# Rotary embedding of queries and keys: one VectorE product with both tables, the halves exchanged by DMA instead of ScalarE, GpSimd left with the sum

## The reference

```python
x = x + xattn(layernorm(x), ctx, ctx, mask, Wq, Wk, Wv, Wo)
x = x + ffn(layernorm(x), w1, w2, w3)

def apply_rope(x):                      # x: (b, t, h, 128)
    inv_freq = 1.0 / 10000.0 ** (arange(0, 128, 2) / 128)
    phase = tile(arange(t)[:, None] * inv_freq[None, :], (1, 2))
    return x * cos(phase) + rotate_half(x) * sin(phase)   # rotate_half: (-x2, x1)

# xattn: x is (8, 128, 512), 32 query heads, 8 key/value heads, 128 wide
q = apply_rope(query @ Wq); k = apply_rope(key @ Wk); v = value @ Wv
logits = 30 * tanh(q.k * 0.088388 / 30); weights = softmax(where(mask, logits, -1e30))
out = (weights @ v) @ Wo
# ffn: w1, w2, w3 are first quantised to the 16 values of NF4 in blocks of 64 and scaled back
out = (silu(x @ dq(w1).T) * (x @ dq(w2).T)) @ dq(w3).T
```

## Time and profile before

| | us |
|---|---|
| median of 3 runs | 922.24 (921.41 to 922.72) |
| the profiled execution's own time | 921.3 |
| its span, first to last instruction | 919.3 |
| busy: PE, PEld | 823.1, 650.1 |
| busy: DVE, ACT, POOL | 679.2, 534.9, 634.7 |
| mean granted TensorE clock | 0.964 of full |

### The profile page before, as it was taken

How to read it: one execution, slowest core, us unless ns; L and a number is a source line. 1 busy time by engine, 2 the same in 40 slices (tenths; PEclk the granted TensorE clock), 3 DMA queues, 4 the chain that set the end, 5 groups by cost and what they waited for, 6 DMA issues and landing times.

```text
span 919.3 us, 10659 instructions
## 1 busy us (share of the span) xinstructions
PE 823.1 (90%) x3806; PEld 650.1 (71%) x3806; DVE 679.2 (74%) x793; ACT 534.9 (58%) x681; POOL 634.7 (69%) x352
## 2 busy tenths in 40 slices
PE   3688798799899899899899899899877899998998
PEld 2467585677677677677677677677555688887886
DVE  8999969487677677677677677687698789896120
ACT  1266478477588488577577577577554266463100
POOL 4778549899899898898898898898720334434000
PEclk9899899799999999999999999999899999999999
DMA  8213453311311311312312212211200310403210
GB/s 315 98 51 115 146 181 108 104 35 46 121 35 47 120 35 49 118 35 56 110 35 70 98 37 82 83 45 44 78 0 32 101 46 3 153 1 100 55 58 35
DMA packets 49140, 70.83 MB, mean 77 GB/s; under 512 B 4160, under 2 KB 25792, under 8 KB 49088
## 3 DMA queue, kind: packets, MB, share of 16 engines
q1 hardware_dynamic: 49088, 70.15, 23.4%
HBM read 51.00 MB, written 19.14 MB: 76 GB/s over the span
## 4 chain that ended last, share of the span: by engine, by line
PE 53%; POOL 20%; DVE 17%; issue 5%; ACT 5%; DMA 0%; POOLq 0%; DVEq 0%; SPq 0%; ACTq 0%
POOL qT L1085 6%; DVE nfa L807 4%; PE bank L397 4%; PE bank L395 4%; PE bank L396 4%; PE bank L415 4%; PE bank L414 4%; PE bank L413 4%; POOL sw L1081 4%; PE bank L429 4%; PE avp L493 4%; PE bank L431 4%; PE bank L430 4%; PE bank L482 3%; PE trp L402 3%
## 5 line engine op out<-in xcount | busy, mean ns | idle before, releaser
L807 DVE SCALAR_TENSOR_TENSOR nfa<-nfp,nfa 128x1408 f32<-128x1408 uint8 x168 | 326.6, 1944 | 99.8 <-ACT nfp L624 98.6
L624 ACT ACTIVATE nfp<-nfv,bnd 128x1408 uint8<-128x1408 f32 x180 | 256.0, 1460 | 61.5 <-POOL nfv L1103 51.1
L1085 POOL TENSOR_TENSOR qT<-qT,sw 128x512 f32<-128x512 f32 x80 | 165.3, 2066 | 34.9 <-DVE qT L814 25.1
L631 ACT ACTIVATE sw<-bank 64x512 f32<-64x512 f32 x80 | 47.5, 594 | 139.5 <-PE bank L415 93.1
L429 PE MATMUL bank<-woh,ath 128*128 128x512 f32 x256 | 110.5, 432 | 0.0
L413 PE MATMUL bank<-xh,wqh 128*128 128x512 f32 x256 | 107.9, 422 | 0.0
L1137 POOL TENSOR_TENSOR eb<-eb,maskf 128x512 f32<-128x512 f32 x64 | 92.6, 1448 | 17.8 <-ACT eb L686 17.8
L431 PE MATMUL bank<-woh,atl 128*128 128x512 f32 x256 | 104.4, 408 | 0.0
L430 PE MATMUL bank<-wol,ath 128*128 128x512 f32 x256 | 104.3, 407 | 0.0
L414 PE MATMUL bank<-xl,wqh 128*128 128x512 f32 x256 | 103.0, 402 | 0.0
L415 PE MATMUL bank<-xh,wql 128*128 128x512 f32 x256 | 103.0, 402 | 0.0
(11 more groups left out here) (120 smaller groups left out, 1664.9 us busy)
## 6 DMA issues: line engine op xcount, KB each, us to landing
dq_scratch<-nfa SPq DMA_DIRECT2D x12, 704.0 KB, 3.1
stage<-wq_pieces SPq DMA_DIRECT2D x32, 256.0 KB, 2.9
stage<-wo_pieces SPq DMA_DIRECT2D x32, 256.0 KB, 2.6
stage<-dq_scratch SPq DMA_DIRECT2D x32, 256.0 KB, 3.2
nfv<-nf_rest SPq DMA_DIRECT2D x7, 704.0 KB, 4.1
ks_scratch<-qT SPq DMA_DIRECT2D x16, 256.0 KB, 2.1
vs_scratch<-vst SPq DMA_DIRECT2D x16, 256.0 KB, 2.4
kcur<-ks_scratch SPq DMA_DIRECT2D x16, 256.0 KB, 2.9
```

Source lines behind the costliest of these rows:

```text
L624: nc.scalar.activation(nfp[:, i % 2, :], nfv[:, :], ACT.Sign, bias=bnd[:, i:i + 1])\
L807: op = nc.vector.scalar_tensor_tensor(nfa[:, :], nfp[:, b % 2, :], STEPS[b], nfa[:, :], ALU.mult, ALU.add)
L1085: nc.gpsimd.tensor_tensor(dst, dst, sw[:, slot, :], ALU.add).then_inc(roped, 1)
```

## The change

- ACT's two copies per unit are gone (160 instructions).
- DVE's `rope_parts` multiplies the PSUM bank by both tables in one instruction, 128 x 2 x 512, into `products`, a new SBUF buffer of two slots (`cs_start` for the keys and the first six queries, `cs_loop` for the rest). It now waits for the bank itself (`proj_done`) and for the sum of the unit two before.
- SP's `swap` waits for the products (`cs_done`) and copies the sine product's halves, exchanged, from SBUF to SBUF into `sw`: two DMAs of 64 partitions x 512, 128 KB each. They stand in SP's one queue, in written order.
- POOL's `rope` waits for both DMAs (32 on the slot's semaphore) and adds the cosine product and `sw` into `qT`. The sine multiplications (80 instructions) are gone. The sign table changes sides, since it is now applied before the exchange.
- Waits that protect `qT` from being overwritten move from DVE to POOL. The key stores and first pieces in SP's queue are written in another order around the swaps.

```diff
-            def cos_part(ru, slot, dst, cos):
-
-                dve.wait_ge(swapped, ru + 1)
-                nc.vector.tensor_tensor(dst.rearrange("p (b t) -> p b t", b=4),
-                                        prj[slot][:, :].rearrange("p (b t) -> p b t", b=4), batches(cos), ALU.mult)\
-                    .then_inc(cos_done, 1)
+            def rope_parts(ru, slot, both):
+
+                dve.wait_ge(proj_done, ru + 1)
+                wait(dve, roped, ru - 1)
+                nc.vector.tensor_tensor(
+                    products(ru, slot).rearrange("p c (b t) -> p c b t", b=4),
+                    prj[slot][:, :].rearrange("p (o b t) -> p o b t", o=1, b=4).to_broadcast([128, 2, 4, S]),
+                    both.rearrange("p c (o t) -> p c o t", o=1).to_broadcast([128, 2, 4, S]), ALU.mult)\
+                    .then_inc(cs_done, 1)
...
-            def swap(ru, slot):
-
-                act.wait_ge(proj_done, ru + 1)
-                wait(act, roped, ru - 1)
-                nc.scalar.activation(sw[0:64, slot, :], prj[slot][64:128, :], ACT.Copy)
-                nc.scalar.activation(sw[64:128, slot, :], prj[slot][0:64, :], ACT.Copy).then_inc(swapped, 1)
...
+            def swap(ru, slot):
+
+                sp.wait_ge(cs_done, ru + 1)
+                wait(sp, roped, ru - 1)
+                part = products(ru, slot)
+                sp.dma_start(sw[0:64, slot, :], part[64:128, 1, :]).then_inc(swapped[slot], 16)
+                sp.dma_start(sw[64:128, slot, :], part[0:64, 1, :]).then_inc(swapped[slot], 16)
...
-            def rope(ru, slot, dst, sin):
-
-                pool.wait_ge(swapped, ru + 1)
-                part = sw[:, slot, :].rearrange("p (b t) -> p b t", b=4)
-                nc.gpsimd.tensor_tensor(part, part, sin.rearrange("p (o t) -> p o t", o=1).to_broadcast([128, 4, S]),
-                                        ALU.mult).then_inc(sin_done, 1)
-                pool.wait_ge(cos_done, ru + 1)
-                pool.wait_ge(sin_done, ru + 1)
-                nc.gpsimd.tensor_tensor(dst, dst, sw[:, slot, :], ALU.add).then_inc(roped, 1)
+            def rope(ru, slot, dst):
+
+                pool.wait_ge(cs_done, ru + 1)
+                pool.wait_ge(swapped[slot], 32 * (ru // 2 + 1))
+                nc.gpsimd.tensor_tensor(dst, products(ru, slot)[:, 0, :], sw[:, slot, :], ALU.add).then_inc(roped, 1)
```

In SP's `head(kv)`, with j = 8 kv:

```diff
                 nf_store(dq3[:, CH:2 * CH] if kv == 0 else dq12[:, (kv - 1) * CH:kv * CH], kv + 1)
-                head_piece(8 * kv + 4)
+                query_swap(j + AHEAD)
+                head_piece(j + 4)
+                query_swap(j + AHEAD + 1)
...
+                head_piece(j + 5)
+                query_swap(j + AHEAD + 2)
+                head_piece(j + 6)
+                query_swap(j + AHEAD + 3)
+                head_piece(j + 7)
...
+                query_swap(j + AHEAD + 4)
+                head_piece(j + 8)
+                query_swap(j + AHEAD + 5)
...
+                head_piece(j + 9)
+                query_swap(j + AHEAD + 6)
+                head_piece(j + 10)
+                query_swap(j + AHEAD + 7)
```

More of the change, by code:

```diff
@@ L119, in build @@
             ctl = sb("ctl", [128, KT, TOK], f32r, context)
+        with ExitStack() as loop:
+            cs_loop = sb("cs_loop", [128, 2, 2, 512], f32, loop)
         sb("ffn_place", [128, 6144])
         woh1 = sb("woh1", [128, G, D], f32r)
+        with ExitStack() as start:
+            cs_start = sb("cs_start", [128, 2, 2, 512], f32, start)
         wol1 = sb("wol1", [128, G, D], f32r)
@@ L179, in build, with products @@
         NF_STEPS = 20
+        def products(ru, slot):
+            return (cs_start if ru < NK + AHEAD else cs_loop)[:, slot, :, :]
         def split(eng, n):
@@ L281, in _ @@
             nf_load(nf_first[:, 0:CH], 0)
+            swap(0, 0)
+            swap(1, 1)
             for n in range(16, 20):
                 first_piece(n)
[L284 to L289, removed]
+            k_store(0)
+            for u in range(2, NK):
+                swap(u, u % 2)
+                k_store(u - 1)
+                if u in (9, 12):
+                    for n in (20, 21) if u == 9 else (22, 23):
+                        first_piece(n)
+            k_store(NK - 1)
             for n in range(24, 28):
@@ L442, in _ @@
                     split(pe, 16)
-                wait(pe, cos_done, u - 1)
+                wait(pe, cs_done, u - 1)
                 cs = slice(half * 512, (half + 1) * 512)
@@ L654, in _ @@
             for u in range(NK):
-                swap(u, u % 2)
                 if 6 <= u < 14:
@@ L696, in head @@
                         high(32 + j)
-                    if j + AHEAD < NUNIT:
-                        swap(NK + j + AHEAD, (j + AHEAD) % 2)
                     if j + 2 < NSTEP:
@@ L1123, in query_rope @@
             def query_rope(u):
-                _, half, g = unit_parts(u)
-                rope(NK + u, u % 2, qT[:, half, g, :], sinq[:, :])
+                kv, half, g = unit_parts(u)
+                if u < 8:
+                    pool.wait_ge(k_out[u], 32)
+                else:
+                    pool.wait_ge(logits_done, 8 * (kv - 1) + 4 * half + 4)
+                rope(NK + u, u % 2, qT[:, half, g, :])
             for u in range(AHEAD):
```

63 lines of the change are left out of this document (27 added, 36 removed).

## The result

| | before | after |
|---|---|---|
| median of 20 runs each | 922.07 us | 919.69 us |
| ratio, 95% interval | | 0.9979, 0.997 to 0.9989 |
| profiled execution, span | 919.3 us | 917.3 us |
| granted clock, mean | 0.964 | 0.972 |
| busy PE, DVE, ACT, POOL | 823, 679, 535, 635 us | 820, 699, 439, 465 us |

A forecast was written before the change was run, and what follows sets the result against it. It took PE and POOL to run level in a head, POOL's order setting most of the head's end. Seven heads at +2.7 (+19), keys 0, first queries -3: +16 on 921.3, so 938 us as median; range 906 to 966.

The forecast's parts named there:

- what is added on SP, and this decides: Swaps on SP in a head's steps: each unit takes 8.4 us against PE's 7.74, so 2.6 us more a head.
- the ring: In a head's steps: low part, piece, two swaps issued and landed, sum, mask, next low part; 8.4 us a unit.
- The head's end: Three stretches from step 5's logits to the second sum behind: 18.9, 11.4 and 6.8 us; changes +1.4, -1.6, +0.3.
- The last head: The head that loads no pieces and projects two units; left out of the +2.7 us booked for each of seven heads.
- Issue of the swaps: SP's time to issue a swap: assumed 0.33 us each, like a piece, with 0.04 between.
- Landing: From the second swap's issue to its landing: taken as 2.1 us, like the key stores, with ends 1.6 and 2.8.
- Keys: Key stage, 18 to 92 us: DVE's longer products against less lengthening by POOL; booked 0, between +8.5 and -10 us.
- First queries: POOL's first masks, for which PE waits 7.32 us, begin at 162.0 instead of 164.69: -3 us (0 to -7).
- no change: Rival: both L807 mostly hide in POOL's gap, 7.7 us a unit, gains and losses at the ends cancel: 922 us, chance 0.07.
- Relief wins: Rival: swaps land in 1.6 us, hidden under PE's step; heads -8, keys -4, first queries -4: 906 us, chance 0.22.
- DVE alone: Rival: nothing comes back in the key stage and heads hide the transfer; +8.5 - 3: 928 us, chance 0.07.
- the rule weighed in the prediction: Skill's rule: two half-partition DMAs gain almost nothing over one after the other; its rival, serial swaps: 972 us, chance 0.14.

The follow-up runs named there:

- e1: The changed kernel with each step's pair of swaps issued on SP behind the piece that waits for that step's low part: 1007.7 us, ratio 1.094.
- e3: The kernel before without POOL's product with the sine (left out of the computation), everything else as it was: 900.2 us, ratio 0.977.
- e12: The kernel before with DVE's cosine product of step 7 made behind the first of its three NF4 adds: 916.8 us, ratio 0.994.
- e9: The changed kernel with DVE's rotation product of step 7 behind the first of its three NF4 adds instead of the second: 902.0 us, ratio 0.978.
- e7: The changed kernel with the halves exchanged by two ScalarE copies instead of the two DMAs, and e9's edit: 1074.8 us, ratio 1.165.

## Why the prediction was wrong

**The step that failed** is the one called "what is added on SP, and this decides": "the piece waits for the low part of the same step", a ring of 8.4 us a unit, +2.6 us a head, +18 in seven heads. The piece that waits for a step's low part stands *behind* that step's swaps; the piece ahead of them waits for the low part of one step earlier, since it refills the slot used four pieces before. The text ahead of the prediction says "three before it" and "in the same step", and is wrong in both. The trace shows it: the swap follows the product by 0.02 us, and SP has sent the piece long before. e1, in which the ring is made, has 9.1 us a unit where the prediction had 8.4, and heads of 80.5 us. From the end of the next head's second sum at 385.73 to the logits of its step 5 at 416.83 are 31.1 us; before, 31.1 too (389.70 to 420.82). Forecast: 2.6 more.

**The head's end was right**, to a few tenths. From the logits of step 5 to the end of step 7's sum: 18.9 forecast, 368.13 - 348.98 = 19.15. To the mask behind the next sum: 11.4 forecast, 11.4 measured. To the next sum's end: 6.8 forecast, 385.73 - 379.50 = 6.2 measured. ACT's planes were to come 0.3 us earlier: from step 5's logits to the add ahead of the product were 365.08 - 352.69 = 12.4 us, now 361.09 - 348.98 = 12.1. Without the ring the prediction's own terms give +0.1 us a head. This head came out at -0.3, the mean of six within 0.1 of none. With the ring left out of the sum, the prediction would have read about 920 us (921.3 + 7 x 0.1 - 3 + 0.9). That this is the time measured is luck in part: the keys gave 1.6 us that were not booked, and the first and the last head lost 1.3 and 2.2 that were not booked either.

**The last head** was left out of the sum, and there the exchange is waited for most plainly. Its second sum starts at 656.62, after 3.02 us of waiting for its transfer, and PE waits for it in turn:

```profile
657.94 2.08 PE L518 MATMUL bank<-qT,kcur 128*128 128x512 f32 x2 [3.12 <-POOL qT L1097]
```

Before, the same wait was 1.48 us.

**The product** was put at 1.21 us: 1.20 to 1.22. **Issue of the swaps** at 0.33 each: 0.46 and 0.60, too low. **Landing** at 2.1, and 3.0 from product to sum: 2.2 to 2.3, and 3.0.

**Keys** were booked at 0: behind them, among the values, the second chunk's maxima start at 114.32 instead of 115.91, so -1.6. DVE is busy 64.4 us in 20 to 92 us, 4 less than the earlier trace rows in spite of 8.5 more of products, so an estimated 12 us of lengthening went, where I had put 9; the estimate is rough, as the window now holds 85 instructions of DVE instead of 80. L833 fell from a mean of 1198 ns to 508 (now L855), the NF4 adds only from 2008 to 1879. But DVE now waits, 4.6 us for the guess and 2.4 for sums:

```profile
35.83 1.30 POOL L1097 TENSOR_TENSOR qT<-cs_start,sw 128x512 f32<-128x512 f32 x1 [5.95 <-DMA sw<-cs_start]
37.08 1.65 POOL L1109 TENSOR_TENSOR guess<-veps,half_neg 128x8 f32<-128x8 f32 x1
```

**First queries**, -3: the masks begin at 160.16 instead of 164.69, 4.5 us earlier, and with 1.6 of it from the keys that is 2.9, as forecast. PE waits 4.97 us for them instead of 7.32. The end of head 0 then gives some of it back (5.1 us ahead in its step 5, 3.8 in that of head 1).

**The rivals.** Nearest was "no change", held at 0.07, by the mechanism that it named in its second half: gains and losses at the ends cancel. "Relief wins" put the head's end at 35.9 us, the forecast at 37.1, and it measured 36.8; it failed on the landing time of 1.6 us, and its -4 for the keys and -4 for the first queries were too much. "DVE alone" had +8.5 us in the keys, where 1.6 were gained. On the rule weighed in the prediction, two DMAs for two halves: the pair landed in 2.2 to 2.3 us each, not one after the other at the price of a whole tile each (2.0 to 2.8, twice); no run has one DMA for both halves, so whether the pair gains anything over one stays open.

## What to carry to other kernels

Ask of a wait in a queue in order what the instruction *behind* it releases: here the sum's 3 us of transfer cost 2 us in each head because a scaling that needed nothing of it stood behind it, and moving that scaling shortened a head by 2.4 (17 us in all, of which the same move gave 12 without the transfer). Before a ring is believed, its members are followed by their counter values over two rounds of the loop, not by their place in one round. And a change that takes work off an engine and puts a wait in its place may be worth little until the order is written anew for it: POOL's relief alone gave 2.3% in the old order (e3), the change gives 0.2% there, and 3.4% with three places moved. Two of these, in like form and each alone in the kernel before, gave 1.3% and 0.6% (both at once, and the third, were not tried there).

## What the runs showed of the hardware

- An SBUF-to-SBUF DMA of 64 partitions x 512 float32 (128 KB) costs the queue 0.46 and 0.60 us of issue for the two of a pair, and lands 2.2 to 2.3 us after; behind a 256 KB piece issued 0.4 us earlier, 2.9.
- A POOL sum and an NF4 add of DVE (L807, L826) stretch each other: 1.27 to 2.5 us on POOL, and the two adds of e12, with sum and mask over them, took 4.43 us against e9's 3.29. Which POOL instruction pays moves with the order: the mean of the 80 sums fell from 2.07 to 1.39 us ((76.0 + 35.0) / 80, with the 22 of the start stage) with the change, the mask's rose from 1.45 to 1.75. DVE's product, which reads PSUM, was never stretched: the 80 of them lie between 1.160 and 1.224 us. The Trainium skill, SBUF — State Buffer, section "SBUF: two separate sides", has DVE instructions with two SBUF inputs and GpSimd's that read SBUF take turns under an exclusive lock; the rows agree, the product (one input in SBUF, one in PSUM) included.
- Behind a wait of PE of 1.86 to 1.88 us the granted clock fell to half in four of six heads of the kernel before; in the other two it did not fall behind such a wait (1.87 us) but behind a later one of 2.2. In the six heads of the changed kernel it fell behind the waits of 1.91, 1.92 and 2.12 us and not behind the nine of 1.85 to 1.89. Twelve matmuls took 4.43 us there instead of 2.83. A head came out no longer for it, as PE's next waits were shorter.
- A ScalarE copy of 64 partitions x 512 float32 from SBUF to SBUF takes 0.63 us (e7), from PSUM it took 0.59 (before).
